# Moving the router's tanh and the transpose of its weights one unit earlier in a four-round mixture-of-experts kernel

## The reference, cut to what matters

```python
x = x + tanh(g_xattn[0]) * cross_attention(layernorm(x), ctx_768, ...)   # x: 16 x 128 x 128
x = x + tanh(g_ffn[0]) * more_forward(layernorm(x), Wg, bg, W1, b1, W2, b2)

B, S, H, F, E, R, TOPK = (4, 256, 128, 512, 4, 4, 2)
cur = x                                              # 2048 tokens of 128
for r in range(R):
    flat = cur.reshape(-1, h)
    logits = flat @ Wg[r] + bg[r]                    # 4 experts
    vals, idx = jax.lax.top_k(logits, TOPK)
    w = jax.nn.softmax(vals, axis=-1)                # weights of the best two
    cw = jnp.sum(jax.nn.one_hot(idx, E) * w[..., None], axis=1)
    hmid = jax.nn.gelu(jnp.einsum('nh,ehf->enf', flat, W1) + b1[:, None, :])
    y = jnp.einsum('enf,efh->enh', hmid, W2) + b2[:, None, :]
    cur = cur + jnp.einsum('ne,enh->nh', cw, y)      # every expert is computed for every token
```

## Time and profile before

| what | value |
|---|---|
| median of 3 runs | 539.15 us (538.98 to 539.61) |
| the profiled execution | 538.98 us, span 537.2 us |
| outside the span | 538.98 - 537.2 = 1.8 us |
| PE busy | 497.2 us, 93% of the span |
| DVE busy | 407.7 us, 76% |
| ACT busy | 373.1 us, 69% |

### The profile page before, as it was taken

One profiled execution on the slowest core, in us unless ns is written; L12 is line 12 of the kernel. 1 busy time (PEld: TensorE's weight loads), 2 busy tenths in 40 slices (PEclk: granted clock), 3 DMA queues, 4 the chain that ended last, 5 costly groups with the idle time before them and its releaser, 6 DMA issues.

```text
span 537.2 us, 8396 instructions
## 1 busy us (share of the span) xinstructions
PE 497.2 (93%) x2529; PEld 402.4 (75%) x2529; DVE 407.7 (76%) x792; ACT 373.1 (69%) x717; POOL 78.7 (15%) x149
## 2 busy tenths in 40 slices
PE   0967998999779999999999999999999999999996
PEld 0945777777567878878888887888788888887884
DVE  3789898889855977697787769768776866876775
ACT  1444556655456887788688778778887877878873
POOL 3374466565300000000000000000000000000000
PEclk9985999999988999999999999999999999999999
DMA  5500000000004012004002100300210040031001
GB/s 135 163 2 0 2 0 0 0 0 0 2 0 159 1 65 94 1 0 159 1 2 83 76 0 1 157 2 0 107 52 1 1 159 0 1 112 67 20 1 39
DMA packets 13063, 22.39 MB, mean 42 GB/s; under 512 B 5200, under 2 KB 9957, under 8 KB 10981
## 3 DMA queue, kind: packets, MB, share of 16 engines
q1 hardware_dynamic: 9648, 21.42, 11.3%
q10 hardware_dynamic: 3381, 0.55, 0.6%
HBM read 20.79 MB, written 1.18 MB: 41 GB/s over the span
## 4 chain that ended last, share of the span: by engine, by line
PE 88%; DVE 6%; ACT 2%; DMA 1%; ACTq 1%; issue 1%; DVEq 0%
PE ps L1121 11%; PE ps L1123 11%; PE ps L1122 11%; PE ps L1101 11%; PE ps L1103 11%; PE ps L1102 11%; PE ps L1015 7%; PE ps L993 4%; PE ps L1002 3%; ACT probT L507 2%; DMA rows_in<-in_L_xattn_bkv_dram 1%; PE ps L949 1%; PE ps L1089 1%; PE ps L1033 1%; DVE v_blk L691 1%
## 5 line engine op out<-in xcount | busy, mean ns | idle before, releaser
L801 DVE TENSOR_TENSOR h_lo<-g_sb,h_hi 128x512 fp32r<-128x512 f32 x256 | 169.8, 687 | 81.2 <-ACT h_hi L597 81.2
L590 ACT ACTIVATE g_sb<-ps,cols 128x512 f32<-128x512 f32 x256 | 175.7, 687 | 75.4 <-PE ps L1103 74.8
L597 ACT ACTIVATE h_hi<-g_sb 128x512 fp32r<-128x512 f32 x256 | 154.1, 631 | 0.0
L1121 PE MATMUL ps<-h_hi,w_hi 128*128 128x512 f32 x256 | 103.5, 404 | 0.0
L1101 PE MATMUL ps<-x_hi,w_hi 128*128 128x512 f32 x256 | 102.2, 399 | 0.8 <-DVE x_lo L795 0.8
L1103 PE MATMUL ps<-x_hi,w_lo 128*128 128x512 f32 x256 | 101.9, 398 | 0.0
L1123 PE MATMUL ps<-h_hi,w_lo 128*128 128x512 f32 x256 | 101.9, 398 | 0.0
L1122 PE MATMUL ps<-h_lo,w_hi 128*128 128x512 f32 x256 | 101.2, 395 | 0.0
L1102 PE MATMUL ps<-x_lo,w_hi 128*128 128x512 f32 x256 | 101.2, 395 | 0.0
L811 DVE SCALAR_TENSOR_TENSOR contrib<-ps,cols,cwb 128x512 f32<-128x512 f32 x64 | 47.8, 746 | 14.0 <-PE ps L1123 8.4
L1101 PEld LDWEIGHTS ps<-x_hi,w_hi 128*128 128x128 f32 x256 | 48.6, 190 | 12.3 <-issue 1.0
(11 more groups left out here) (129 smaller groups left out, 504.1 us busy)
## 6 DMA issues: line engine op xcount, KB each, us to landing
cwb<-cw_rows SPq DMA_DIRECT2D x16, 1024.0 KB, 5.7
x_sb<-in_x_dram SPq DMA_DIRECT2D x4, 256.0 KB, 8.8
w_in<-in_L_ffn_W_dram SPq DMA_DIRECT2D x1, 1024.0 KB, 7.9
out_dram<-xn SPq DMA_DIRECT2D x4, 256.0 KB, 2.3
ctx_sb<-in_ctx_dram ACTq DMA_DIRECT2D x1, 462.0 KB
cw_rows<-cwT SPq DMA_DIRECT2D x8, 16.0 KB, 1.4
wq_in<-in_L_xattn_Wq_dram SPq DMA_DIRECT2D x1, 64.0 KB, 2.7
bv_row<-in_L_xattn_bkv_dram ACTq DMA_DIRECT2D x1, 64.0 KB, 9.1
```

The costliest lines, as they stand in the source:

```text
L590: nc.scalar.activation(g_sb[:, k, :], ps[:, k, :], ACT.Gelu_apprx_tanh, bias=b1_c[:, e * NF + k:e * NF + k + 1]).then_inc(gelu_done, 1)
L597: nc.scalar.activation(h_hi[:, u % 2, k, :], g_sb[:, k, :], ACT.Copy).then_inc(hi_done, 1)
L801: nc.vector.tensor_tensor(h_lo[:, u % 2, k, :], g_sb[:, k, :], h_hi[:, u % 2, k, :].bitcast(F32), ALU.subtract).then_inc(lo_done, 1)
L1121: mm(yb, w2_hi[:, w], hh, start=k == 0, stop=False)
```

## The change

Of the pairs 1 to 7, ACT's `gate(q)` goes from round 3 to round 2, that is from behind `hidden(4)` to behind `hidden(3)` (units counted from the pair's first). `transpose_weights(q)` on PE and `move_cwT(q)` on ACT go from round 5 to round 4. The instructions, their number and their sizes stay. DVE's list stays as it is: `router(q)` in round 2, `weights(q)` in round 3. So does SP's list.

```diff
@@ block.scalar, lines 635 to 638 @@
-                if q < PAIRS and u % (2 * E) == 3:
+                if q < PAIRS and u % (2 * E) == 2:
                     gate(q)
-                if q < PAIRS and u % (2 * E) == 5:
+                if q < PAIRS and u % (2 * E) == 4:
                     move_cwT(q)
```

## The result

| | before | after |
|---|---|---|
| median of 4 runs | 539.38 us (538.98 to 539.74) | 546.33 us (545.48 to 546.67) |
| ratio, 95% interval | | 1.0127 (1.0109 to 1.0144) |
| the profiled execution | 538.98 us, span 537.2 | 545.69 us, span 544.0 |

The change makes the kernel 1.3% slower, 6.95 us by the medians and 6.8 us by the two spans. The forecast was 545.6 us in a range from 543.5 to 548.1.

The account below looks back on a forecast made before the run. PE was taken to bound the mixture of experts. Seven PE stalls of 0.94 us make 6.6 us, taking the profiled execution from 538.98 to 545.6 us, in a range from 543.5 to 548.1.

Parts of the forecast that it names:

- PE bounds the mixture of experts, nothing earlier on ACT or DVE can gain: Mixture of experts: PE is never late for data, so making ACT's or DVE's results ready earlier cannot shorten the span.
- The gate waits 3.5 us: ACT, pairs 1 to 7: the gate behind hidden(3) waits for half_d, 3.5 us each time.
- The burst behind it runs as in pair 0: ACT's hidden(4) behind the waiting gate runs dense: h2 3.33 us after g0, h3 ending 4.49 us after it.
- cw ends 5.86 us after half_d: Chain from half_d through gate, hidden(4), low and weights to cw on ACT and DVE: 5.9 us, cw ready at 189.08.
- PE stands still for 0.94 us: PE behind up(5), seven pairs: the transpose waits for cw from 188.19 to 189.13, 0.94 us each, 6.6 us in sum.
- Bank 3 of up(5) has 0.66 us of room: PE in up(5): bank 3 is needed at 187.50 and g3 ends at 186.84, so PE doesn't wait there.
- the rival: ACT's burst comes 0.66 us later, catching bank 3 of up(5) too: stalls 1.4 us or more, 548.8 up, chance 0.08.
- ACT catches up in one or two units: ACT starts hidden(5) at about 187.8 instead of 186.29; the lag is gone one or two units later.
- The two moves only cost together: Gate or transpose left in its old place: cw is early by 0.9 or 4.7 us, so no PE wait.
- Copy and DMAs cost nothing: move_cwT, store and two broadcasts go about 5.6 - 0.94 us earlier; they gain nothing and cost nothing.
- The clock holds at 1.00: PE's granted clock stays 1.00 after 170 us; the rival, a fall behind each stall, gave 557, chance 0.05.
- the 1.7 us of the prediction: Cost of the half-clock stretch from 163.4 to 166.8 us after pair 0's long wait: 3.4 x 0.49 = 1.7 us.

Follow-up runs that it names:

- e1_gate_only: Kernel before with only the gate moved to round 2, transpose and copy left in round 5: 538.72 us, ratio 0.9996.
- e5_router_long: Changed kernel with three more instructions in the router on DVE, 0.96 us more from the logits to half_d: 552.93 us, ratio 1.0278.
- e10_router_longer: Changed kernel with nine more instructions in the router on DVE, 2.9 us more: 570.94 us, ratio 1.0596.
- e2_transpose_only: Kernel before with only the transpose and the copy moved to round 4, gate left in round 3: 539.13 us, ratio 1.0005.
- e3_copy_late: Changed kernel with the copy of the transposed weights, and so the store and broadcasts, put back to round 5: 546.81 us, ratio 1.0146.
- e7_first_down_ahead: Kernel before, but in pair 0 PE issues down(0) ahead of the transpose instead of behind it: 535.44 us, ratio 0.9943.
- e4_behind_down: Changed kernel, but PE issues the round 4 transpose behind down(4) instead of ahead of it: 538.36 us, ratio 0.9990.
- e9_weights_first: Changed kernel, but DVE does weights(q) at the start of round 3, ahead of low(4,0), not behind low(4,3): 538.17 us, ratio 0.9991.

## Why the prediction was right, point by point

- *PE bounds the mixture of experts, nothing earlier on ACT or DVE can gain.* Right: no experiment on the pairs 1 to 7 was faster than before beyond its interval, and `e1_gate_only`, with 25 us of new waits on ACT, was the same.
- *The gate waits 3.5 us.* Measured 3.55.
- *The burst behind it runs as in pair 0.* h2 was put 3.33 us after g0; it came 186.31 - 182.98 = 3.33 after.
- *cw ends 5.86 us after half_d.* Measured (188.40 + 0.27) - (182.62 + 0.19) = 5.86.
- *PE stands still for 0.94 us.* Measured 0.96 to the transpose. The term was slightly undersized by what comes behind: `down(4)` starts 0.10 us after the transpose, where 0.03 was the distance to `down(5)` in its old place (193.82 against 193.79 on the timeline of before). With that a pair costs 1.01 us, and seven of them 7.1 instead of 6.6. This 0.5 us, and the 0.4 by which the median of before (539.38) lies over the execution that the forecast started from (538.98), make 0.9; the median after lies 0.7 over the forecast. That the profiled execution came within 0.1 us of the forecast, 545.69 against 545.6, is in part luck: it came to the loop 0.4 us earlier than that of before, which hides most of the 0.5.
- *Bank 3 of up(5) has 0.66 us of room.* Right: in the changed kernel no PE wait on `gelu_done` is in its list, and in `e5_router_long`, with 0.96 us more, bank 3 is 0.30 us late. In `e10_router_longer`, with 2.9 us more, bank 0 stops PE first and bank 3 again behind it: the rival was right that the banks are next, and had not looked at so large a delay.
- *ACT catches up in one or two units.* `hidden(5)` follows at once at 187.35, and `hidden(6)` waits for PE again at 192.61.
- *The two moves only cost together.* Shown by `e1_gate_only` and `e2_transpose_only`.
- *Copy and DMAs cost nothing.* Shown by `e3_copy_late`.
- *The clock holds at 1.00.* Right for stalls of 1.0, 2.0 and, split in two, 3.9 us a pair. The argument for it was weaker than it looked. The prediction counted one fall of the clock in the mixture of experts, but its trace has another, at `up(0)`: 0.52 from 149.8 to 153.2 us, right behind a stretch from 146 to 149.8 in which PE was busy for 1.57 of 3.8 us. The stretch that the prediction held against a fall, from 144 to 147.4, ends only 2.4 us ahead of it. That stalls of 1 us in dense work leave the clock alone is shown by the changed kernel, not by those rows.

## What to carry to other kernels

Before an instruction with a wait is moved ahead, compare two times: when what it waits for is ready, and when its engine gets to the new place; then ask the same of every waiting instruction further down the chain, with its producers at their new times, since two moves that are free one by one can cost together. A small instruction that waits stops the whole queue behind it, so on the engine that sets the pace it belongs behind work whose inputs are already there; `e7_first_down_ahead` gained 3 us in this way, by its profile less than half of it from the filled gap itself and the rest from the clock, which stayed up. And a wait in a place that was already slow (here pair 0) is the best measure of what the same wait will cost elsewhere.

## What was not expected of the hardware

After pair 0's wait of 3.4 us the granted clock fell in the profiles of the kernel before, the changed kernel, `e1_gate_only`, `e2_transpose_only` and `e4_behind_down` (0.88 from 158 to 172 us), but not in those of `e3_copy_late` and `e9_weights_first`, whose pair 0 has the same instructions and the same wait. The two rows, in this order:

```profile
158.00:172.00 14.00, 10.61 (x55) 1.00 0.16 55
```

```profile
158.00:172.00 14.00, 10.61 (x56) 1.00 0.22 83
```

In `e9_weights_first`, which has no PE wait in its list between pair 0 and the end of the loop, the loop time is 372.57 - 371.07 = 1.50 us shorter than before: that is what the fall costs, against the 1.7 us of the prediction. In `e3_copy_late` the loop time is only 379.66 - 378.98 = 0.68 us shorter than in the changed kernel (its span is longer, 544.9 against 544.0, because it came to the loop 1.67 us later). The rest is given back at pair 1. PE comes there earlier against DVE, whose `share(0)` waits for the broadcast of `cwb` as before; the first of its seven waits for `cw` is 1.3 us instead of 0.8, and bank 3 of `up(5)` is 0.26 us late:

```profile
PE ps L1110 <- DVE cw L876: 6.0, 7, 1.3
```

So the same wait was followed by the fall in five profiles and not in two. What decides it was not tested, nor how often it happens in the runs without a profile.
